# Two transformer layers on one core: the standard deviations of q and k spread through DRAM, and some work in other slots

## The reference

```
mod = silu(cond) @ w_mod + b_mod            # shift, scale, gate for attention and for the MLP
h   = layernorm(x) * (1 + scale) + shift
q, k, v = split(h @ w_qkv + b_qkv)          # 16 heads of 18 channels
q, k = layernorm over the 18 channels of each head, times g_q, g_k      # layer 0 only
o   = softmax(q k^T / sqrt(18)) v           # 256 x 256 scores for each head
x   = x + gate * (o @ w_proj + b_proj)
h   = layernorm(x) * (1 + scale2) + shift2
x   = x + gate2 * (gelu(h @ w1 + b1) @ w2 + b2)      # hidden width 1152
```

## Time and profile before

| | us |
|---|---|
| median of 3 runs (lowest, highest) | 2635.77 (2634.47, 2638.5) |
| the profiled execution's own time | 2637.22 |
| its span | 2635.4 |
| PE busy | 2497.1 (95%) |
| DVE busy | 1835.8 (70%) |
| ACT busy | 1570.4 (60%) |
| POOL busy | 671.5 (25%) |

### The profile page before, as it was taken

One profiled execution on the slowest core, in us unless ns is written; L12 is line 12 of the kernel. 1 busy time (PEld: TensorE's weight loads), 2 busy tenths in 40 slices (PEclk: granted clock), 3 DMA queues, 4 the chain that ended last, 5 costly groups with the idle time before them and its releaser, 6 DMA issues.

```text
span 2635.4 us, 59209 instructions
## 1 busy us (share of the span) xinstructions
PE 2497.1 (95%) x22440; PEld 2107.0 (80%) x22440; DVE 1835.8 (70%) x3702; ACT 1570.4 (60%) x2861; POOL 671.5 (25%) x937
## 2 busy tenths in 40 slices
PE   5669999999999999999999999999999999999998
PEld 3447888888888888888887788888888888888878
DVE  5557777777777777777776777676677667777664
ACT  3356666666666666666655656565656555565553
POOL 2113223223223223223222222221222222122122
PEclk9779999999999999999999999999999999999999
DMA  5574653553453553553653654455355445544531
GB/s 138 93 177 87 106 89 67 86 89 67 86 90 66 87 90 66 86 89 63 119 89 76 132 89 74 81 94 83 77 83 96 79 75 89 90 79 79 86 59 41
DMA packets 210153, 229.91 MB, mean 87 GB/s; under 512 B 20984, under 2 KB 197344, under 8 KB 209360
## 3 DMA queue, kind: packets, MB, share of 16 engines
q1 hardware_dynamic: 197564, 196.13, 44.3%
q10 hardware_dynamic: 12308, 30.00, 3.8%
HBM read 88.50 MB, written 28.12 MB: 44 GB/s over the span
## 4 chain that ended last, share of the span: by engine, by line
PE 67%; SPq 11%; DMA 9%; DVE 8%; issue 5%; POOL 0%; ACT 0%; DVEq 0%; POOLq 0%; ACTq 0%
PE psum L736 16%; PE psum L834 8%; DMA attn_k_stack<-attn_qk_hi 7%; SPq L1307 7%; PE psum L907 5%; PE psum_exp L736 5%; PE psum_max L736 5%; PE psum_exp L810 5%; PE psum L909 5%; PE psum L908 5%; PE psum_max L823 4%; SPq L1312 3%; DVE attn_maxima L1084 3%; PE psum L743 2%; PE psum L797 1%
## 5 line engine op out<-in xcount | busy, mean ns | idle before, releaser
L945 ACT ACTIVATE attn_probs<-psum_exp 128x1024 f32<-128x1024 f32 x512 | 524.2, 1024 | 437.3 <-PE psum_exp L810 433.2
L1084 DVE TENSOR_REDUCE attn_maxima<-psum_max 128x4 f32<-128x1024 f32 x512 | 622.0, 1215 | 140.2 <-PE psum_max L823 134.1
L1253 POOL TENSOR_TENSOR mlp_x<-mlp_x,mlp_gated 128x288 f32<-128x288 f32 x128 | 102.8, 803 | 1168.3 <-DVE mlp_gated L1101 1168.3
L907 PE MATMUL psum<-mlp_w_fc_hi,mlp_hidden_hi 128*128 128x288 f32 x1152 | 346.7, 301 | 17.0 <-DVE attn_o_split L1169 14.9
L736 PE MATMUL psum<-attn_ln_split,w_qkv_split 128*128 128x256 f32 (+3 forms) x2240 | 340.9, 295 | 1.8 <-ACT attn_ln_modulated L759 1.0
L909 PE MATMUL psum<-mlp_w_fc_hi,mlp_hidden_lo 128*128 128x288 f32 x1152 | 339.9, 295 | 0.0
L908 PE MATMUL psum<-mlp_w_fc_lo,mlp_hidden_hi 128*128 128x288 f32 x1152 | 339.7, 295 | 0.0
L736 PEld LDWEIGHTS psum<-attn_ln_split,w_qkv_split 128*128 128x128 f32 (+3 forms) x2240 | 281.6, 181 | 52.4 <-issue 16.3
L834 PE MATMUL psum<-attn_probs,attn_v 128*20 128x256 f32 x4096 | 277.5, 389 | 1.1 <-ACT attn_probs L945 1.1
L810 PE MATMUL psum_exp<-attn_q_stack,attn_k_stack 64*128 64x256 f32 x2048 | 259.3, 332 | 13.3 <-DMA attn_q_stack<-attn_neg_max_lo 12.2
L823 PE MATMUL psum_max<-attn_k_stack,attn_q_stack 62*128 62x256 f32 x2048 | 215.2, 289 | 59.0 <-DMA attn_k_stack<-attn_qk_hi 50.1
(11 more groups left out here) (178 smaller groups left out, 4413.3 us busy)
## 6 DMA issues: line engine op xcount, KB each, us to landing
attn_q_stack<-attn_qk_hi SPq DMA_DIRECT2D x256, 128.0 KB
attn_k_stack<-attn_qk_hi SPq DMA_DIRECT2D x256, 128.0 KB
mlp_gate_and_gated_bias<-modulation ACTq DMA_DIRECT2D x64, 288.0 KB, 3.3
attn_q_stack<-attn_qk_lo SPq DMA_DIRECT2D x128, 128.0 KB
attn_k_stack<-attn_qk_lo SPq DMA_DIRECT2D x128, 128.0 KB
attn_x<-in_x_dram SPq DMA_DIRECT2D x32, 288.0 KB, 7.3
attn_gate<-modulation SPq DMA_DIRECT2D x64, 144.0 KB, 3.4
mlp_x<-in_x_dram SPq DMA_DIRECT2D x32, 288.0 KB, 3.7
```

The lines of the kernel that those rows point to most:

```text
L907: q.matmul(bank[:, 0:C], h_hi[:, c, cols], w2_hi[:, c, :], start=(c == 0), stop=False)
L945: q.activation(probs[r][:], ps_exp[:], ACT.Exp, scale=SCORE_SCALE).then_inc(S["exps"], 1)
L1084: q.tensor_reduce(maxes[g % 2][:, p // QUARTER, :, p % QUARTER, :], ps_max[:].rearrange("p a (t n) -> p a t n", t=TT), AX.X, ALU.max).then ...
L1253: q.tensor_tensor(xt, xt, gated2[:], ALU.add).then_inc(S["added2"], 1)
```

## The change

- **Deviations.** The two parts, the matrix `head_spread`, its set-up and the ten matmuls L881 and L882 of a unit are gone. `rs_raw` is written to DRAM (one DMA of 128 KB) and read back onto the rows of all channels into `sq_sb`, whose squares are used up by then (two DMAs, 64 KB and 512 KB). All three stand in SP's queue in slots 6 and 7; the second and third wait for the first to land. DVE's multiplication reads `sq_sb` in SBUF and waits for both reads before the first chunk.
- **Slots in layer 0.** The chunks 1, 2 and 3 of q and k move to slots 1, 2 and 3, the sum of squares from slot 8 to slot 4, v from slots 5 and 7 to 7 and 8. DVE's multiplications stay where they were (slots 12 to 15).
- **The maxima's turn** moves one slot ahead in both layers, to slots 11 and 3, and with it DVE's and SP's steps behind it.
- **Second half of the second MLP product**, in layer 1 only, moves from slot 9 to slot 13, the load of its gate from slot 14 to slot 0.
- **Once only.** The MLP weights of layer 0 are arranged from ACT's queue at the start; those of layer 1 and the modulation weights of layer 1 move in several smaller DMAs.

```diff
-CHUNK_AT = {4: (-34, -26), 0: (-33, -23), 1: (-30, -22), 2: (-29, -20), 3: (-26, -18)}
-VALUE_AT = [(-27, -29), (-25, -17)]
-VAR_AT = -24
-SPREAD_AT = {4: -21, 0: -20, 1: -19, 2: -19, 3: -18}
+CHUNK_AT = {4: (-34, -26), 0: (-33, -23), 1: (-31, -22), 2: (-30, -20), 3: (-29, -18)}
+VALUE_AT = [(-25, -29), (-24, -17)]
+VAR_AT = -28
+RSTD_OUT, RSTD_IN = -26, -25
+QK_Y = {4: -20, 0: -19, 1: -18, 2: -18, 3: -17}
-MAX_AT, MAX_TR = -12, -4
+MAX_AT, MAX_TR = -12, -5
-STATS2, RSTD2, NORM2, REST2, TR2, Y2, SPLIT2, GATE2_AT = 31, 32, 35, 36, 37, 38, 39, 46
-FC1_AT, FC2_AT, STORE_AT = 49, [51, 57], 68
+STATS2, RSTD2, NORM2, REST2, TR2, Y2, SPLIT2, GATE2_AT = 31, 32, 35, 36, 37, 38, 39, (46, 48)
+FC1_AT, FC2_AT, STORE_AT = 49, [(51, 51), (57, 61)], 68
...
-MOD_REST_AT, MOD_TR, MOD_STORE, MOD_LOAD = (-25, 11), (-19, 13), (-13, 15), -11
-ARRANGE_AT = (-27, 55, 71)
+MOD_REST_AT, MOD_TR, MOD_STORE, MOD_LOAD = (-25, 11), (-19, 13), (-13, 15), (-11, -9, -7, -3, -1, 1)
+ARRANGE_AT = (55, 57, 71, 73, 87, 89)
...
+        rstd_d = scratch("qk_rstd", (32, 4, N))
...
 def prep_act(q):
...
+            q.wait_ge(S["raw_loaded", 0], 16 * RAW_MOVES)
+            for part in range(6):
+                arrange(q, 0, part)
...
 # DVE
-                    if (g := due(T, SPREAD_AT[c] + 1, [0])) is not None:
+                    if (g := due(T, QK_Y[c], [0])) is not None:
                         z = z_sb[0:rows_c, c, :]
-                        q.wait_ge(S["spread_mm"], NQK * g + i + 1)
...
+                        if i == 0:
+                            q.wait_ge(S["rstd_in"], 32 * (g + 1))
+                            q.wait_ge(S["qk_z"], NQK * (g + 1))
...
-                        q.scalar_tensor_tensor(out=z, in0=z, scalar=qk_gain[0:rows_c, c:c + 1], in1=psum[banks["spread", g, c][0]][0:rows_c, 0:N],
+                        q.scalar_tensor_tensor(out=z, in0=z, scalar=qk_gain[0:rows_c, c:c + 1], in1=sq_sb[0:rows_c, c, :],
                                                op0=ALU.mult, op1=ALU.mult).then_inc(S["qk_y"], 1)
...
-                if (g := due(T, VAR_AT + 2, [0])) is not None:
-                    q.wait_ge(S["rs_exp"], g + 1)
...
-                    q.tensor_copy(rs_hi[:], rs_raw[:]).then_inc(S["rs_hi"], 1)
-                    q.wait_ge(S["rs_hi"], g + 1)
-                    q.tensor_tensor(rs_lo[:], rs_raw[:], fp(rs_hi[:]), ALU.subtract).then_inc(S["rs_lo"], 1)
...
 # SP
+                if (g := due(T, RSTD_OUT, [0])) is not None:
+                    q.wait_ge(S["rs_exp"], g + 1)
+                    if g > 0:
+                        q.wait_ge(S["rstd_in"], 32 * g)
+                    q.dma_start(rstd_d.rearrange("r c n -> c r n"), rs_raw[:]).then_inc(S["rstd_out"], 16)
+                if (g := due(T, RSTD_IN, [0])) is not None:
+                    q.wait_ge(S["rstd_out"], 16 * (g + 1))
+                    q.dma_start(sq_sb[0:4 * TAIL, 4, :], rstd_d[0:TAIL].rearrange("r c n -> c r n")).then_inc(S["rstd_in"], 16)
+                    q.dma_start(sq_sb[:, 0:4, :].rearrange("p c n -> p (c n)"),
+                                rstd_d[0:PAIRS].rearrange("(o s) c n -> o s (c n)", o=1).broadcast_to([MAIN_D, PAIRS, 4 * N])).then_inc(S["rstd_in"], 16)
```

More of the change, by code:

```diff
@@ L182, in bank_table @@
         for c in QK_ORDER:
-            if (g := due(T, SPREAD_AT[c], [0])) is not None:
-                take(("spread", g, c), T, T + 1.9)
             if (g := due(T, CHUNK_AT[c])) is not None:
@@ L531, in mod_row @@
                 part = MOD_FIRST.index(n)
[L532 removed]
+                q.wait_ge(S["w_mod_loaded", part], MOD_LOADED[part])
             q.wait_ge(S["mod_mm"], n + 1)
@@ L669, in new_weights, with arrange @@
             q.dma_start(fp(dst[0:LAST_ROWS, 4, :]), w_new_d[0:LAST_ROWS, 4, cols]).then_inc(signal, 16)
[L672 to L678 removed]
+        def arrange(q, l, part):
+            w, bias, second = MLP_NAMES[l]
+            if part < 2:
+                q.dma_start(w1_d[l][:, part, :], a[w][P * part:P * part + P, :]).then_inc(S["w1_arranged", l], 16)
+            elif part == 2:
+                for dst, src in last_moves(w1_d[l][:, 2, :], a[w], a[bias].rearrange("(o n) -> o n", o=1), slice(0, MLP)):
+                    q.dma_start(dst, src).then_inc(S["w1_arranged", l], 16)
+            else:
+                c = 3 * (part - 3)
+                q.dma_start(w2_d[l][:, c:c + 3, :], a[second][P * c:P * c + 3 * P, :].rearrange("(c p) n -> p c n", p=P)).then_inc(S["w2_arranged", l], 16)
         def load_w1(q, l):
@@ L875, in slots_pe @@
                 for c in QK_ORDER:
-                    if (g := due(T, SPREAD_AT[c], [0])) is not None:
-                        q.wait_ge(S["rs_lo"], g + 1)
-                        if g == 0:
-                            q.wait_ge(S["spread_ready"], NQK)
-                        bank = bank_of(("spread", g, c))
-                        q.matmul(bank[0:QK_ROWS[c], 0:N], spread[:, c, 0:QK_ROWS[c]], rs_hi[:], start=True, stop=False)
-                        q.matmul(bank[0:QK_ROWS[c], 0:N], spread[:, c, 0:QK_ROWS[c]], rs_lo[:], start=False, stop=True).then_inc(S["spread_mm"], 1)
                     if (g := due(T, CHUNK_AT[c])) is not None:
@@ L996, in slots_act @@
                             q.activation(parts[0][0:rows_c, c, :], bank[0:rows_c, 0:N], ACT.Copy).then_inc(S["part_hi", 1], 1)
-                    if (g := due(T, SPREAD_AT[c] + 2, [0])) is not None:
+                    if (g := due(T, QK_Y[c] + 1, [0])) is not None:
                         q.wait_ge(S["qk_y"], NQK * g + i + 1)
@@ L1033, in slots_act @@
                     split_proj_hi(q)
-                if T == ARRANGE_AT[1]:
-                    arrange_w1(q, 1)
-                if T == ARRANGE_AT[2]:
-                    arrange_w2(q, 1)
+                for part, at in enumerate(ARRANGE_AT):
+                    if T == at:
+                        arrange(q, 1, part)
                 if T in STAGE_AT:
@@ L1093, in slots_dve @@
                         q.tensor_tensor(gated[:], psum[banks["proj", g, t][0]][:, 0:C], gate[:], ALU.mult).then_inc(S["gated"], 1)
-                    if (g := due(T, FC2_AT[t] + 1)) is not None:
+                    if (g := due(T, after(FC2_AT[t], 1))) is not None:
                         n = TT * g + t
@@ L1249, in slots_pool @@
                         q.tensor_tensor(xt, xt, gated[:], ALU.add).then_inc(S["attn_added"], 1)
-                    if (g := due(T, FC2_AT[t] + 2)) is not None:
+                    if (g := due(T, after(FC2_AT[t], 2))) is not None:
                         xt, n = xr[g % XR_RING][:, t, :], TT * g + t
@@ L1275, in slots_pool @@
                 for i, c in enumerate(QK_ORDER):
-                    if (g := due(T, SPREAD_AT[c] + 3, [0])) is not None:
+                    if (g := due(T, QK_Y[c] + 2, [0])) is not None:
                         rows_c = QK_ROWS[c]
```

106 lines of the change are left out of this document (43 added, 63 removed).

## The result

The changed kernel takes 2604.8 us (median of four runs, 2600.2 to 2611.2) against 2636.9 (2634.5 to 2638.5): ratio 0.988, 95% interval 0.986 to 0.990. It is 1.2% faster, by 32 us, where 55 were forecast. Its profiled execution took 2611.2 us with a span of 2609.3, against a span of 2635.4 before, so 26 us are to be explained in the traces; this execution is the slowest of the four, 6 us over their median.

What follows compares the result with a forecast made beforehand. PE was taken as the bound (784.34 of 790 us busy in layer 0, 923.78 of 950 in layer 1). 2637.2 - 33 (layer 0) - 26 (layer 1) + 5 (once only) = 2583, against the median 2582 us; range 2548 to 2630.

Steps and rivals of the forecast that it cites:

- Start, +5: Before the steady units: slower way through DRAM to the first stack and modulation-weight DMAs cost 5 us, between -1 and +10.
- Layer 0, -33: Layer 0: removed spreading matmuls and their wait, less new waits, gain 1.05 us a unit, 33 us over 31 distances.
- (a): Layer 0, slot 11: PE waits about 0.3 us at the turn for the reduction of slot 10's pair.
- (b): Layer 0, DVE's chain to slot 0's maxima: multiplications from SBUF contend with POOL, 0.7 us taken; PE gets 1.6 there.
- (c): Layer 0, slot 8: v's second half waits about 0.55 us for the bank that DVE's L1169 empties.
- The way through DRAM, 9.9 us with 2 to spare: Layer 0: deviations' write and reads take 9.9 us of 12 until chunk 4 needs them, estimated from nearest store and load rows.
- Layer 1, -26: Layer 1: waits for DVE's L1169, stacks and negatives go, less 0.15 at the turn; net 0.85 us a unit, 26 us.
- several us more for the stacks: Layer 1: 27 matmuls (3.6 us) in slot 13 give SP time, removing stack and negatives waits, 0.46 us a unit.
- The waits (a) to (c) do arise: Rival, layer 0: these waits do not arise, as DVE's order leaves the reductions early enough; 2549 us, chance 0.17.
- the contention is 0.8 of its full 2.0 us: Rival, layer 0: DVE and POOL hold each other up in full, four multiplications taking 0.51 more; 2624 us, chance 0.15.
- the way through DRAM is fast enough: Rival: the way through DRAM is too slow, DVE stands at chunk 4 in slot 12; 2675 us at 15 us, chance 0.12.
- wrong if: Signs against the forecast: DVE waits for `attn_qk_squares` each unit, layer 0 units over 39.5 apart, layer 1 keeps stack waits.

Runs made afterwards that it cites:

- y2_slot15: Changed kernel with two gate buffers, gate load in slot 8, half product in slot 15 (unit 61's in 9), plus chunk 2's layer 0 multiplication one slot later: 2566.2 us.
- value_slot5: gate_ring_46 with the first half of v of layer 0 back in slot 5, its second half left in slot 8: 2593.2 us.
- gate_ring_46: Changed kernel with two buffers for the second MLP half's gate, its load in layer 1 back in slot 14 instead of slot 0: 2583.1 us.
- before_turn: Kernel before with only the turn of the maxima one slot earlier: 2619.5 us.
- fc2_back: Changed kernel with the layer 1 part undone: second MLP product's second half back in slot 9, its gate load in slot 14: 2603.1 us.

## Why the prediction was right in kind and half wrong in size

The time, 2604.8, lies in the range 2548 to 2630, and "faster" was given 0.85. The forecast's 2582 is 23 us too low; in the profiled executions it is 28 (2611.2 against 2583), and the parts show where.

- **Start, +5:** measured +4.4. DVE waits for the reads only there. The part scatters by more than its size among the kernels, so this is no proof of the term.
- **Layer 0, -33:** measured -29.4. Spreading matmuls and their wait are gone. No kernel has this step alone: by the table it takes the earlier turn and the spreading together, either alone gives 7. (a) 0.3 us at the turn: 0.2 (4.2 us in 20.5 units). (b) 0.7 of contention out of bounds of 0 to 2.0: 0.8, of which chunk 4's multiplication has 0.2 and chunk 2's 0.56, and PE waits 0.3 at slot 0; y2_slot15 shows that this chain does hold the unit. (c) 0.55 in slot 8: 0.43. Not forecast: 0.55 us at L740, since v no longer covers ACT's modulation in slot 5; value_slot5 shows that it costs nothing while (b) stands.
- **The way through DRAM, 9.9 us with 2 to spare:** from the end of ACT's exponential to the last packet of the reads 8.7 us (7.9 to 9.5 over units 5 to 30), with 3.3 to spare (2.5 to 4.1). DVE's 12.0 us of time was right to 0.1. The nearest rows were too high: SP issues the write at 784.60 and the first read, which waits for it, at 788.18, 3.6 us later, where the store's row says 5.0. By the rule in the Trainium skill, DMA: Bandwidth & Descriptors, section on why a DMA increments its semaphore by 16, the write would run on 4 engines; if it does, 3.6 us is what that costs here, and nothing waits for it.
- **Contention:** the Trainium skill, GPSIMD Engine Reference, section Specifications, says that GpSimd and VectorE contend for their SBUF interfaces, and names instructions with two SBUF inputs. The trace agrees for two of the four multiplications, those of chunks 4 and 2; the other two overlap POOL's L1262 and last 0.47 and 0.48 us: the one at 798.36 had started before it, the one at 799.24 starts 0.18 us before its end. The prediction's "it does not run until POOL's instruction is through" is too strong: L1208 before and both held multiplications here end 0.27 to 0.29 us behind POOL's, less than the 0.43 to 0.48 that each takes alone.
- **Layer 1, -26:** measured -1.1. **The step that failed is "the new place of the product's gate load and of POOL's adds costs nothing, since the store is five slots behind".** It looked at who needs the gate, and not at what the transfer collides with on the DMA engines: +23.4 us. Without it, gate_ring_46 gives 24.5 in layer 1, near the 26, and in part by luck: its units gain 1.13 us in place of 0.85, and the end, which the forecast left out, loses some 6. A second step is wrong and was covered: SP was said to have "several us more for the stacks" by the matmuls in slot 13. They lie ahead of slot 14, where the stacks' way begins; the wait for the stacks went because of the earlier turn (0.4 us in before_turn, which has nothing else; 0.3 in fc2_back and gate_ring_46).
- **The end:** not in the sum, and 6 us lost there. The moved half no longer covers the last unit's wait for the split, 3.7 us; the rest was not taken apart.
- **The turn** stood in layer 0's sum only as a cost, 0.3 a unit, and in layer 1's as 0.15 against the 0.2 of the negatives' wait. As part of this change it is what makes it pay, 29 us; the sum was not hurt, since it took the negatives to be in time.

No rival happened. The waits (a) to (c) do arise; the contention is 0.8 of its full 2.0 us; the way through DRAM is fast enough. The last condition under "wrong if", that layer 1 keeps its waits for the stacks, is what came true.
